# Masked cross attention: GpSimd clears masked exponentials in four of eight key blocks, where TensorE added a mask product to the scores

## What is computed

```
scores = (q @ k.T) / sqrt(16)              # 512 queries x 1024 keys
scores = where(mask != 0, scores, -inf)    # one mask (512 x 1024) for all heads and rows
out    = softmax(scores) @ v
```

## Time and profile before

| | |
|---|---|
| median of 3 runs | 4087.71 us (4085.89 to 4091.82) |
| span of the profiled execution | 4082.7 us |
| TensorE, matmuls busy | 3805.6 us, 93% |
| VectorE busy | 2426.6 us, 59% |
| ScalarE busy | 1752.6 us, 43% |
| GpSimd busy | 152.0 us, 4% |

### The profile page before, as it was taken

The page is one execution under the profiler, slowest core; times in us unless marked ns, Lnnn a source line. Parts: engine busy times, 40 slices in busy tenths (PEclk is TensorE's granted clock), DMA queues, the critical chain, the costliest instruction groups (busy, mean ns, idle before and its releaser), DMA issues.

```text
span 4082.7 us, 59517 instructions
## 1 busy us (share of the span) xinstructions
PE 3805.6 (93%) x22502; PEld 1826.4 (45%) x22502; DVE 2426.6 (59%) x6081; ACT 1752.6 (43%) x3256; POOL 152.0 (4%) x168
## 2 busy tenths in 40 slices
PE   4999899999999989999999998999999999899999
PEld 2353444345435244435544524443553443444355
DVE  5568576843366856683237676767333776676642
ACT  1755434531274643462128374336113836433611
POOL 1000020000000002000000001100000000200000
PEclk9999999999999999999999999999999999999999
DMA  5313002133331200203342210130435121012043
GB/s 174 128 43 63 19 17 52 25 111 127 115 119 34 54 19 24 57 13 129 128 137 90 40 38 19 44 50 1 148 109 163 63 52 26 19 46 48 1 164 98
DMA packets 152763, 286.26 MB, mean 70 GB/s; under 512 B 25317, under 2 KB 84709, under 8 KB 147557
## 3 DMA queue, kind: packets, MB, share of 16 engines
q1 hardware_dynamic: 152456, 282.22, 24.1%
HBM read 187.49 MB, written 44.30 MB: 57 GB/s over the span
## 4 chain that ended last, share of the span: by engine, by line
PE 76%; DVE 17%; ACT 4%; issue 2%; PEldq 1%; SPq 0%; DMA 0%; PEld 0%; DVEq 0%; POOLq 0%; ACTq 0%
PE ps L1257 11%; PE ps L589 7%; PE ps L572 6%; PE ps L1286 5%; PE ps L412 5%; DVE mx L755 4%; PE ps L516 4%; PE ps L1676 3%; PE ps L1573 3%; PE ps L577 3%; PE ps L1614 3%; PE ps L468 2%; PE ps L1597 2%; DVE ps L752 2%; PE ps L620 2%
## 5 line engine op out<-in xcount | busy, mean ns | idle before, releaser
L693 ACT ACTIVATE PT<-ps 128x512 f32<-128x512 f32 (+2 forms) x1280 | 643.8, 564 | 324.5 <-PE ps L577 174.7
L1257 PE MATMUL ps<-xnT,f_w 128*128 128x512 f32 x1088 | 489.7, 593 | 0.0
L755 DVE TENSOR_REDUCE mx<-ps 128x1 f32<-128x512 f32 (+3 forms) x768 | 430.7, 617 | 75.4 <-PE ps L516 38.3
L572 PE MATMUL ps<-QS,KS 99*128 99x512 bf16 (+2 forms) x1280 | 419.0, 368 | 9.2 <-ACT PT L693 8.7
L516 PE MATMUL ps<-KS,QS 96*128 96x512 bf16 (+3 forms) x1280 | 391.6, 367 | 17.4 <-DVE mx L755 6.9
L752 DVE CUSTOM_DVE_ANT_0 ps<-ps,mneg 128x512 f32<-128x512 f32 x512 | 340.7, 718 | 82.2 <-PE ps L516 79.1
L589 PE MATMUL ps<-PT,VP 128*32 128x512 f32 (+3 forms) x2560 | 371.1, 573 | 0.0
L412 PE MATMUL ps<-mneg,identb 128*128 128x512 bf16 x1200 | 314.6, 388 | 28.9 <-DVE a_fin L1791 10.9
L1380 DVE TENSOR_TENSOR f_tm<-f_si,ps 128x512 f32<-128x512 f32 x128 | 88.0, 687 | 426.2 <-ACT f_si L1332 425.9
L1332 ACT ACTIVATE f_si<-ps 128x512 f32<-128x512 f32 x136 | 81.3, 597 | 584.2 <-PE ps L1257 584.2
L1257 PEld LDWEIGHTS ps<-xnT,f_w 128*128 128x128 f32 x1088 | 205.5, 190 | 201.4 <-issue 195.2
(11 more groups left out here) (282 smaller groups left out, 5584.1 us busy)
## 6 DMA issues: line engine op xcount, KB each, us to landing
f_w<-in_wF SPq DMA_DIRECT2D x136, 384.0 KB, 3.1
ctxT<-weight_rows SPq DMA_DIRECT2D x120, 256.0 KB, 3.4
scores<-a_fin SPq DMA_DIRECT2D x64, 256.0 KB, 3.0
a_fin<-scores SPq DMA_DIRECT2D x32, 512.0 KB, 4.3
a_Y<-in_wA SPq DMA_DIRECT2D x5, 3072.0 KB, 14.7
KS<-KP SPq DMA_DIRECT2D x240, 64.0 KB, 2.3
scores<-a_fin SPq DMA_DIRECT2D x64, 192.0 KB, 3.0
a_fin<-scores SPq DMA_DIRECT2D x12, 1024.0 KB, 7.6
```

The costliest lines, as they stand in the source:

```text
L572: last = nc.tensor.matmul(o, m["KS"][0:KST, h, j * P:(j + 1) * P], m["QS"][0:KST, h, q0:S], start=True, stop=plain)
L693: nc.scalar.activation(m["PT"][:, mp % 2, j % 2, e, 0:w], ps[:, SLOTS + n % TURNED, 0:w], ACT.Exp, scale=HD ** -0.5).then_inc(g("exp"), 1)
L755: nc.vector.tensor_reduce(m["mx"][:, h % 2, i, f // BANK:f // BANK + 1], ps[:, k % SLOTS, 0:w], AX.X, ALU.max, negate=True).then_inc(g("sl ...
L1257: last = nc.tensor.matmul(ps[:, 2 * v + e % 2, :], m["w"][:, e % NRING, (2 * v + k) * P:(2 * v + k + 1) * P], xnT[:, k, :], start=(k == 0) ...
```

## The change

In stage E the first four key blocks (`NCAP`) are "capped". Their turned scores get no mask matmul, so the first matmul closes the bank. ScalarE takes the exponential of the unmasked score. GpSimd then multiplies the bits of each exponential, read as a 32-bit integer, with a table of 0 and 1 in place, and `weighted` waits for that as well, by a semaphore `cap` (that of stage B's casts). The table `keepT` (128x2048, from `mnegT`) is formed by GpSimd once a round in the free slot of `wbuf`. A round has 64 such products of 128x512 (8 head pairs, 4 blocks, 2 heads), two in each step from t = 0 to 31: the early pair's where t mod 8 is 0 to 3, the late pair's where it is 4 to 7. Blocks 4 to 7 keep the mask matmul.

```
--- before.py
+++ after.py
@@ -151,6 +151,10 @@
 
     def first_step(self, m):
         return m * self.half
+
+    def capped(self, j):
+
+        return self.masked and j < NCAP
 
     def turn(self, t):
 
@@ -184,6 +188,7 @@
 
 NH = 16
 HD = 16
+NCAP = 4
 NE, NSH = 32, 2
 WARM_LN, WARM_T, WARM_STACK = 22, 6, 3
 WARM_ROUND, WARM_CLEAR = 12, 8
@@ -308,6 +313,7 @@
                           "m_parts", "m_mm", "m_row", "st_mm", "exp", "pv", "o_up", "recip", "y_mm"):
 
                     sm[c, n] = sm["B", n] if c == "D" and "B" in STAGES else sem(f"{n}_{c}")
+        sm["E", "cap"] = sm["B", "cast"]
 
 
         def scope(fn):
@@ -338,6 +344,7 @@
             return m
 
         M16 = scope(attn16_mem)
+        keepT = wbuf[:, 0, 0:NCAP * S].rearrange("p (j q) -> p j q", j=NCAP).bitcast(I32)
 
         WIDTH = {"B": 2560, "D": 3584, "E": 2560, "C": 3616}
         ORDER = [s for s in "BCDE" if s in STAGES]
@@ -443,6 +450,15 @@
             vp = M16["VP"][:, 0:c.nj, :, :].rearrange("p j h d -> p (j h) d")
             ch.link(nc.gpsimd.memset(vp[:, :, HD:32], 0.0))
             nc.gpsimd.memset(vp[:, :, HD:HD + 1], 1.0).then_inc(sm[c.name, "v_zero"], 1)
+            if c.masked:
+                ch.link(nc.gpsimd.tensor_scalar(keepT, mnegT[:, 0:NCAP, :], 0.0, None, ALU.is_equal))
+                for t in range(c.steps):
+                    for x, (mp, j) in enumerate(c.pairs_at(t)):
+                        if c.capped(j):
+                            for e in range(2):
+                                pool.wait_ge(sm[c.name, "exp"], 2 * (c.turn(t) + x) + e + 1)
+                                w = M16["PT"][:, mp % 2, j % 2, e, :].bitcast(I32)
+                                nc.gpsimd.tensor_tensor(w, w, keepT[:, j, :], ALU.mult).then_inc(sm[c.name, "cap"], 1)
 
         def a16_pe(pe, c, n):
             m = M16
@@ -570,15 +586,18 @@
                     o = ps[:, SLOTS + n % TURNED, 0:S - q0]
                     h = 2 * mp + e
                     last = nc.tensor.matmul(o, m["KS"][0:KST, h, j * P:(j + 1) * P], m["QS"][0:KST, h, q0:S],
-                                            start=True, stop=plain)
+                                            start=True, stop=plain or c.capped(j))
                     if c.causal:
                         last = nc.tensor.matmul(o[:, 0:P], identb[:, :], causT[:, :], start=False, stop=True)
-                    if c.masked:
+                    if c.masked and not c.capped(j):
                         last = nc.tensor.matmul(o, identb[:, :], mnegT[:, j, :], start=False, stop=True)
                     last.then_inc(g("st_mm"), 1)
 
             def weighted(t):
                 pe.wait_ge(g("exp"), 2 * c.turn(t + 1))
+                if c.masked:
+                    done = sum(2 * c.capped(j) for x in range(t + 1) for _, j in c.pairs_at(x))
+                    pe.wait_ge(g("cap"), done)
                 for mp, j in c.pairs_at(t):
                     if j == 0 and mp >= 2:
                         pe.wait_ge(g("o_up"), mp - 1)
```

## The result

The changed kernel takes 4153.09 us (median of 4 runs, 4149.33 to 4156.28) beside 4088.22 us for the kernel before on the same chip (median of 4). The ratio is 1.016, with a 95% interval of 1.0145 to 1.0174: 65 us slower, where 16 us were forecast and 4140 was the upper end. The profiled execution took 4156.28 us, its span is 4154.3, and its mean granted clock is 0.975 (before: 0.987). In the profiled executions the four rounds of stage E, from the first score matmul to the last weighting, are longer by 16.6, 16.3, 16.3 and 18.8 us. Stage B, which the change does not touch, adds another 4: it takes 115.3, 116.6, 115.3 and 118.5 us in the four rounds, 115.3 to 115.8 before. One of the seven executions of experiment 9 took 8417.20 us at a mean granted clock of 0.416 and is not in its ratio.

A forecast was written before the change was run, and what follows sets the result against it. TensorE was taken as the bound (busy 95.08 of 95.40 us), with VectorE's chain ending together with it at L554. Savings and holds summed to -4.0 us a round, 16 over four: 4087.7 + 16, say 4103 us, range 4055 to 4140.

The forecast's parts named there:

- early behind early: Three double steps a round: product and L726 tie, +0.43 if won, -0.60 if lost; half taken, -0.25 us in all.
- early behind late: Three double steps a round, GpSimd still on the previous pair: -1.84 lost, -0.85 won; half taken, -4.0 us in all.
- there all 0.88 come: Denominator and normalization steps: TensorE has other work ahead of L554, so the double step's whole 0.88 us saving arrives.
- What is removed, ideally: Stage E without mask matmuls: double steps of 7.84 us become 7.41 (early) or 7.40 (late).
- What is added, the product: GpSimd's 64 products a round: 1.06 to 1.46 us each, 1.15 taken.
- What is added, the collision: GpSimd products hold two-SBUF-input VectorE operations L761, L724, L726 ahead of L554 until they end; tiles' work not held.
- "lost" case: Early pair behind a late one, L724 losing to a product: chain held twice, L554 at 6.96, -1.84 us.
- Costed at nothing: Table behind L445 (at most 5.8 us), TensorE's extra wait instructions, DMA, and granted clock staying 1.00: no cost.
- rival 4: GpSimd becomes the bound, from about 1.9 us a product: 4140 to 4290 us, chance 0.10.
- Rival 1: Four-element VectorE operations are not held, or slip through: +7.9 us a round, 4056 us, chance 0.20.
- rival 2: GpSimd product at the low row, 1.06 us: -0.4 us a round, 4089 us, chance 0.18.
- Rival 3: GpSimd product near 1.3 us: -12.6 us a round, 4138 us, chance 0.14.

The follow-up runs named there:

- experiment 9: Changed kernel with GpSimd's second product in even steps held until the row maxima, and only 40 products a round: 4076.28 us, ratio 0.9967.
- experiment 4: Changed kernel plus twelve extra matmuls into an unused bank in TensorE's waits at steps 1, 9, 17 and 25: 4131.25 us, ratio 1.0098.
- experiment 1: Changed kernel without the 256 GpSimd products and TensorE's wait for them, blocks 0 to 3 left unmasked, table still built: 4066.01 us, ratio 0.994.
- experiment 8: Changed kernel with products of 128x256 in place of 128x512, the other queries left unmasked: 4075.82 us, ratio 0.9968.
- experiment 3: Changed kernel with each product replaced by a GpSimd memset of the same length, which only writes, and no table: 4128.31 us, ratio 1.0096.
- experiment 12: Changed kernel with products in even (early) head pairs only, late pairs keeping TensorE's mask matmuls: 4097.87 us, ratio 1.0021.

## Why the prediction was right and wrong

Both columns are us per round, gain positive, by the prediction's own measure, from b to b (the first score matmul of an even step; 754.25 is one in the changed kernel). The clock's row is what experiment 4 gains over the changed kernel in the double steps 9, 11, 17, 19, 25 and 27, and the rows of those steps are read from experiment 4. It is the first round.

| double steps, by their odd step | predicted | measured |
|---|---|---|
| start, up to step 3 | -1.4 | -4.0 |
| late plain (5, 7) | -0.5 | -0.6 |
| late, denominators (13, 21) | +0.8 | +0.2 |
| late, normalization (15, 23) | +1.8 | +0.8 |
| early behind early (11, 19, 27) | -0.25 | +1.4 |
| early behind late (9, 17, 25) | -4.0 | -6.6 |
| clock behind the long waits | 0 | -7.3 |
| tail | -0.35 | -0.5 |
| sum | -4.0 | -16.6 |

Four such rounds make 66 us, the result. Without the clock's row it is -9.3, or 4125: inside the range. In the other rounds the same loss lies elsewhere: the clock's row is -4.4, -4.5 and -6.9 there, 23 us with the first, and the start's is -5.3, -5.2 and -6.1. Stage E's 68 us less 23 give 4133, still inside.

So the step that failed is the one that costed the clock at nothing; behind it stand the holds, too small in the start and in the early steps behind late ones, and "there all 0.88 come".

- **What is removed, ideally: right for plain steps, wrong for one term.** Experiment 1 has 7.35 to 7.38 for 7.40 and 7.41. "There all 0.88 come" is refuted by the same run: 0.51 with the denominators, 0.44 with the normalization, because TensorE waits for VectorE's tiles ahead of other operations as well. That took 1.6 us a round from the sum.
- **What is added, the product: mis-sized.** "I take 1.15, nearer to the row of the same size" was the wrong choice inside a right range: 1.23 from start to start, 1.27 alone. The row with two full operands was the one to scale: twice 0.73, less one fixed part of 0.19 (experiment 8), is 1.27. By itself the size cost little in the late steps (L570 at b + 5.85, 5.82 forecast, the double step 8.15 for 8.10) and more behind a late pair: b + 7.33 for 6.96. The Trainium skill (GPSIMD Engine Reference, Elementwise side-by-side cycle accounting) has about 2.6 cycles an element for two inputs; the rows agree, with 0.54 us for 256 elements, or 2.5 cycles at 1.2 GHz. That figure by itself is an estimate of 1.11 us for 512; the 1.25 of the prediction holds a fixed part that it does not name.
- **What is added, the collision: the mechanism right, its reach too short.** Maxima above 1 us beside untouched medians, and the wait at L570, came as forecast, and the tiles' work L771 is not held (692 to 736 ns, 690 to 734 before). That only L761, L724 and L726 are held, and the casts L723 and L725 pass, was the mistake; experiment 3 shows the casts held on their own account. In the start L742 took 1.12 us and L743 1.17, one behind the other, and TensorE waited 3.23 us. And early behind late lost each time, twelve of twelve, not half of the times: 2.21 us at full clock, where the "lost" case, also with two whole products in the chain, had 1.84. The ties of early behind early went the other way, three of three won, and experiment 12 shows that they are no ties when GpSimd is not behind.
- **Costed at nothing, the clock: wrong, and the largest miss.** "The granted clock is 1.00 in both windows, the first of which has TensorE waits of over 1 us" was read as leave for waits of 3 us, more than twice the longest of those rows. Behind the wait that ends at 761.58 the clock is 0.60 from 763.60 to 767.00; a double step that the sum has at 7.4 takes 7.75 to 7.85, and the one with the wait up to 12.39 instead of 10.06. Experiment 4 shows it as a cost of its own: the holds stay, matmuls fill the waits, the clock is 1.00 and 22 us come back.
- **Costed at nothing, the rest: right.** The table takes 5.38 us (5.8 at most forecast), and the round's first L570 comes at 717.30 against 717.28 although it runs beside VectorE's work on K: the idle time covers it. TensorE's extra waits show nowhere in the late plain steps, which are 0.05 us from the sum. No capacity limit (rival 4): TensorE's wait for GpSimd is in the tail only, 1.3 us a round.
- **The rivals.** Rival 1 falls by the maxima of 1.2 us, rival 2 by the product's 1.23. Rival 3, a product near 1.3, came nearest with 4138; its -2.6 each for early behind late and -2.0 for the start were the better sizes, its -0.78 for early behind early was not. Its nearness is in part luck: it has nothing for the clock. What no rival had is the second cost of a wait, the clock behind it. Two slips in the sums bear on nothing: 4087.7 + 16 is 4103.7, and two holds of 2 us in 14 chains would be 224 us over four rounds, not 150.

Open: how the start's loss divides between holds and clock, since experiment 4 moved the low clock from step 1 to step 3 and did not take it away; and what decides when the clock falls. The length of the wait alone does not: in experiment 1 the clock is 0.79 around a wait of 1.28 us and in the kernel before 1.00 around one of 1.26. Of the twelve waits of 3.02 us in the changed kernel, ten have a clock of 0.50 or 0.66 in the 5 us behind them and two, at step 9 of rounds 2 and 3, have 1.00. And in stage B, which is the same code, the same wait of 1.22 us is followed by either. These are the 5 us behind it in rounds 3 and 4 of one execution of the changed kernel (columns as in the windows above, the clock third from the end):

```profile
2378.49:2383.49 5.00, 4.62 (x21) 1.23 (x22) 4.57 (x8) 1.68 (x3) 0.00 (x0) 1.00 0.28 67
3401.80:3406.80 5.00, 5.00 (x14) 1.28 (x15) 2.63 (x5) 1.54 (x3) 0.00 (x0) 0.50 0.29 68
```

Products in the early pairs 2, 4 and 6 alone, which experiment 12 suggests, were not tried.

## What to carry to other kernels

Before work goes to an idle GpSimd, list the short VectorE operations that TensorE waits for, casts and copies as much as those with two SBUF inputs: each can cost one whole GpSimd instruction (0.18 us became 1.2 here), so the length of that instruction and where it lies matter more than GpSimd's load. Price a wait of TensorE twice, for its length and for the clock that may fall behind it, above all where the sum has waits longer than any that the trace shows. Two parts that cost -25 and +36 us alone cost +65 together, so price them in the state that they make together.

## What the runs showed of the hardware that was not expected

- Casts of 4 elements a partition are held by a GpSimd instruction that only writes (1.07 and 1.16 us), while two-input operations between them pass in 0.16.
- A 128x512 product on GpSimd takes the same time for integer and float (1272 and 1270 ns); the one of stage C, with a broadcast operand, takes 1058.
- Behind a TensorE wait of 2.7 us the granted clock was 0.50 from 738 to 740 (experiment 4), and four matmuls behind waits of 3.02 and 3.23 us took 0.59 us instead of 0.39. With twelve matmuls in the waits at steps 9, 17 and 25 it did not fall.
- The same code with the same wait of 1.22 us (stage B) is followed by a clock of 1.00 in some rounds and of 0.50 to 0.69 in others (mean of 5 us); a round of stage B takes from 115.3 to 118.5 us with it.
